# Sixteen unrolled attention batches against a loop over twelve of them

## The chip, the cores and the metric

The kernel runs on one core of one Trainium2 chip. The metric is the device time of one execution in microseconds (us). The engines are PE (matrix multiply; its weight loads are listed as PEld), DVE (vector), ACT (scalar and activation), POOL (GpSimd) and SP (which issues the DMAs). A q behind an engine's name (DVEq) means its sequencer: waits, register operations and branches.

## The reference, cut to what matters

The input x is 16 batches of 256 tokens by 256 features. The first half of the block is attention with 16 heads of 128: queries from x, one shared key and value projection scaled per head by a cumulative sum of decayed coefficients, rotary embedding, a causal softmax, and an output projection. The second half is a feed-forward part with 1024 hidden features whose weights are quantised to three values per group of 64.

```python
x = L0_attn_x                                  # (16, 256, 256) float32
x = x + _layernorm(attn(_layernorm(x), Wq, Wkv, Wkvh, Wg, Wout))
x = x + _layernorm(ffn(_layernorm(x), w_gate_up, w_proj))
# attn, for each batch and each of 16 heads of 128:
#   k = rope(kp * kh[head]);  v = vp * vh[head];  q = rope(x @ Wq.T)
#   o = softmax(mask(q @ k.T / sqrt(128))) @ v;   return o @ Wout.T
# ffn: h = silu(x @ Wg.T) * (x @ Wu.T);  return rms_norm(h) @ Wp.T
#   with Wg, Wu, Wp = ternary_quant(...), once for all batches
```

## The kernel before

The work is a hand-written software pipeline. Each of the five engines has its own program, and they meet only through semaphores that count up: an engine waits until a count has reached a threshold.

The attention part goes over 128 steps, eight for each of the 16 batches; a step takes one pair of heads (`HP` = 2, `PAIRS` = 8). Within a step every stage works on a different pair, behind by `LAG`: the projection of the queries (PE), their product with the cosine (DVE, L1372) and the swap of their halves (ACT, L1078 and L1079) on the newest pair; the product with the sine (POOL, L564), the sum (POOL, L574) and the scores (PE, L815 and L817) one behind; the row maxima come from DVE (L1384 to L1387); the exponentials (ACT, L1090 and L1092), the reciprocal of their sums (DVE, L1397) and the normalising product (POOL, L596) two behind; the transposes (PE, L832) with their split into a high and a low part (ACT L1108, DVE L1410) three, the product with the values and its split (ACT L1118, DVE L1419) four, and the output projection (PE, all split products are issued at L710) five behind. POOL also scales the keys (L585). Once per batch come the layer norms of the next batch's input and of the previous one's output, and the projections of keys, gates and values (`FRONT`, `TAIL`). SP loads, two steps ahead, one pair of coefficient rows into `kh_all`.

Beside this the ternary weights are made in six chunks; one chunk takes two batches (`ROUND` = 16 steps), with its stages at the steps listed in `WSTEP`. `chunk_at` says whether a stage of a chunk falls in the present step: `par` is the batch's parity, and the chunks lie in batches 1 to 12.

`over_batches` is called by every engine with its own function `batch(g0, par, steps)`, which writes out that engine's instructions for eight steps; `g0` is the number of the batch's first step. All thresholds and addresses are worked out from `g0` when the program is built: with a Python integer they are constants. The engine helper `pair_at` gives the pair of a stage and `at_least` drops waits that are trivially true.

The feed-forward part goes over 16 units, one per batch. `over_units` writes out the first and last of them and puts the ones between into a loop of the engine (`Fori`, L357), four rounds of two units, whose thresholds come from a register. Its first units run inside the last attention steps. L1142 (ACT, silu) and L1513 (DVE, product of gate and up) are steps of it, L958 is its transpose on PE, and L1533 a statistics operation on x tiles that are addressed by the unit's number.

Of the kernel before, what the change touches and what calls it, by code (L numbers as in the profile page):

```python
# [41 lines left out]
PAIRS = H // HP  # L42
STEPS = BATCH * PAIRS
# [24 lines left out]
WSTEP = dict(cast=0, sum=1, scale=2, above=3, below=3, decide=7, sign=7, change=9, finish=11, turn=15, copy=15, store_chunk=15, next_load=13)  # L68
CHUNKS = 6
ROUND = 2 * PAIRS  # L70
# [6 lines left out]
def sandwich_kernel(nc, x, wq, wkv, wkvh, wg, wout, wgu, wproj, rope, out):  # L77
    ctx = ExitStack()
    with ctx:
# [240 lines left out]

        def chunk_at(g0, par, s, stage):

            if isinstance(g0, int) and not PAIRS <= g0 < PAIRS + CHUNKS * ROUND:
                return None
            if WSTEP[stage] == s + (0 if par else PAIRS):
                return g0 if par else g0 - PAIRS

        def chunks_done(c0, of=1):
# [2 lines left out]

        def over_batches(eng, batch):

            for g0 in range(0, STEPS, PAIRS):
                batch(g0, g0 // PAIRS % 2, PAIRS)
            batch(STEPS, 0, DRAIN)

# [72 lines left out]
        def _(sp):  # L410
# [75 lines left out]
            for p in range(1, KH_LEAD):  # L486
                spread_kh(0, p)
            sp.dma_start(X[:, 2 * NT:half, :], tile_rows[:, 2 * NT:half, :]).then_inc(x_half, 16)
            over_batches(sp, batch)

            out_rows = out.rearrange("b (t p) e -> p (b t) e", p=P)
# [15 lines left out]
        def _(pool):  # L507
# [190 lines left out]
            queries_sin(0, LAG["rope"])  # L698
            queries_add(0, LAG["rope"])
            over_batches(pool, batch)  # L700
            over_units(pool, step)


        @block.tensor
        def _(pe):
# [168 lines left out]
            def weights_turn(g0, par, s):  # L874

                c0 = chunk_at(g0, par, s, "turn")
                if c0 is not None:
                    b = F_BANK.bitcast(BF16)
                    pe.wait_ge(wt_done, chunks_done(c0))
                    pe.wait_ge(v_lo_done, g0 + ROUND)  # L880
                    for a in range(FF // P):
                        last = nc.tensor.transpose(b[:, a * P:(a + 1) * P], w_tern[:, a * P:(a + 1) * P], ident_bf[:, :])
                    last.then_inc(wt_turned, ROUND)
# [116 lines left out]
            for i in range(2, LATER):  # L1000
                turn_weight(i)
            project_keys(0, 0)
            over_batches(pe, batch)
            over_units(pe, step)

# [712 lines left out]
```

## Time and profile before

| | |
|---|---|
| median of 3 runs | 1116.36 us (1114.75 to 1117.43) |
| profiled execution | 1116.36 us |
| its span, first to last instruction | 1114.6 us |
| PE, PEld busy | 95%, 90% |
| POOL, ACT, DVE busy | 84%, 78%, 75% |
| granted TensorE clock | 0.994 of full speed |

The profile is of one execution. A group's row names the line, the engine, what is written from what, and the times; the idle time of an engine stands with what ended it. The span is nearly the whole time; 1.8 us lie around it. Attention takes the first 890 us, the feed-forward part the rest.

### The profile page before, as it was taken

The numbers are of one execution on the slowest core, as the hardware profiler recorded it, in microseconds if no ns is written. First come the engines' busy times: TensorE is split into PE (matmuls) and PEld (weight loads), VectorE is DVE, ScalarE is ACT, GpSimd is POOL, SyncE is SP. The second block draws the span as 40 slices with busy tenths as digits, with TensorE's granted clock in tenths as the row PEclk, the third lists the DMA queues.
The fourth block names the chain that finished last, engine by engine and source line by source line (L and its number), as shares of the span: only waits on it lengthen the run. The fifth ranks groups of instructions, "written<-read, shape, count | busy, mean of one in ns | idle before, by whom it ended". The sixth has DMA issues, their size and how long they took to land.

```text
span 1114.6 us, 25542 instructions
## 1 busy us (share of the span) xinstructions
PE 1060.9 (95%) x8010; PEld 1007.1 (90%) x8010; DVE 841.2 (75%) x2854; ACT 866.7 (78%) x2386; POOL 933.7 (84%) x846
## 2 busy tenths in 40 slices
PE   6899999999999999999999999999999899999997
PEld 6799899889988999899989999999999799999997
DVE  5778887878788878887878897878777756566654
ACT  4887879787878797878888888888888767666674
POOL 3788989898899889988998899989898757767675
PEclk8999999999999999999999999999999999999998
DMA  7450112111111121111111111111131000000001
GB/s 256 163 165 27 50 50 65 36 43 59 50 39 44 53 58 40 39 50 58 39 44 44 67 40 58 43 45 39 39 106 30 1 2 21 21 19 19 19 20 39
DMA packets 35117, 58.46 MB, mean 52 GB/s; under 512 B 3137, under 2 KB 16001, under 8 KB 34689
## 3 DMA queue, kind: packets, MB, share of 16 engines
q1 hardware_dynamic: 34992, 56.96, 16.2%
q8 instruction: 59, 0.97, 0.3%
q14 instruction: 66, 0.53, 0.2%
HBM read 50.92 MB, written 9.18 MB: 54 GB/s over the span
## 4 chain that ended last, share of the span: by engine, by line
POOL 33%; PE 29%; issue 19%; DVE 11%; ACT 7%; DMA 1%; DVEq 0%; POOLq 0%; ACTq 0%
PE psum L710 10%; POOL arena L564 9%; PE psum L899 8%; POOL arena L574 8%; POOL arena L585 7%; POOL arena L596 7%; PE psum L929 4%; DVE pt_split L1410 2%; PE psum L815 2%; ACT arena L1090 2%; ACT arena L1092 1%; DVE arena L1372 1%; DVE o_lo L1419 1%; PE psum L817 1%; PE psum L909 1%
## 5 line engine op out<-in xcount | busy, mean ns | idle before, releaser
L596 POOL TENSOR_TENSOR arena<-arena 128x768 f32<-128x768 f32 x128 | 209.5, 1637 | 24.3 <-DVE arena L1397 23.7
L564 POOL TENSOR_TENSOR arena<-arena,tables 128x512 f32<-128x512 f32 x128 | 170.4, 1331 | 48.8 <-ACT arena L1079 48.1
L1410 DVE SCALAR_TENSOR_TENSOR pt_split<-psum,vh_col,pt_split 128x256 fp32r<-128x256 f32 (+1 forms) x512 | 186.9, 404 | 0.0
L574 POOL TENSOR_TENSOR arena<-arena 128x512 f32<-128x512 f32 x128 | 171.2, 1337 | 10.0
L585 POOL TENSOR_TENSOR arena<-arena 128x512 f32<-128x512 f32 x128 | 170.5, 1332 | 2.2 <-ACT arena L1054 1.8
L815 PE MATMUL psum<-arena 128*128 128x256 f32 x512 | 153.5, 381 | 11.1 <-POOL arena L574 10.9
L710 PE MATMUL psum<-wo_hi,o_hi 128*128 128x256 f32 x512 | 152.7, 298 | 0.0
L1078 ACT ACTIVATE arena<-psum 64x512 f32<-64x512 f32 x128 | 76.2, 595 | 97.7 <-DVE arena L1372 96.5
L1090 ACT ACTIVATE arena<-arena 128x256 f32<-128x256 f32 x256 | 129.5, 506 | 22.4 <-DVE arena L1387 17.5
L710 PE MATMUL psum<-xt_hi,wq_hi 128*128 128x256 f32 x512 | 146.3, 286 | 0.0
L710 PE MATMUL psum<-xt_lo,wq_hi 128*128 128x256 f32 x512 | 144.9, 283 | 0.0
L710 PE MATMUL psum<-xt_hi,wq_lo 128*128 128x256 f32 x512 | 144.7, 283 | 0.0
L710 PE MATMUL psum<-wo_hi,o_lo 128*128 128x256 f32 x512 | 144.4, 282 | 0.0
L710 PE MATMUL psum<-wo_lo,o_hi 128*128 128x256 f32 x512 | 143.7, 281 | 0.0
L710 PE MATMUL psum<-pt_split,vals_hi 128*128 128x512 f32 (+1 forms) x512 | 142.0, 358 | 1.2 <-DVE wo_lo L1268 1.2
L899 PE MATMUL psum<-xt_hi,wq_hi 128*128 128x256 f32 x512 | 128.3, 289 | 1.6 <-DVE xt_lo L1595 1.4
L899 PE MATMUL psum<-xt_lo,wq_hi 128*128 128x256 f32 x512 | 124.6, 282 | 0.0
L1108 ACT ACTIVATE pt_split<-psum,vh_col 128x256 fp32r<-128x256 f32 x256 | 121.6, 475 | 0.0
L1397 DVE RECIPROCAL arena<-arena 128x8 f32<-128x8 f32 x128 | 24.9, 194 | 123.6 <-ACT arena L1092 122.1
L602 POOL TENSOR_TENSOR wo_lo<-arena,wo_hi 128x512 fp32r<-128x512 f32 x64 | 88.8, 1396 | 27.9 <-ACT wo_hi L1149 27.8
L817 PEld LDWEIGHTS psum<-arena 128*128 128x128 f32 x512 | 97.1, 190 | 13.3
L1385 DVE CUSTOM_DVE_ANT_0 arena<-psum,mask 128x256 f32<-128x256 f32 x256 | 106.1, 415 | 0.0
(170 smaller groups left out, 3542.1 us busy)
## 6 DMA issues: line engine op xcount, KB each, us to landing
arena<-kh_rows SPq DMA_DIRECT2D x127, 256.0 KB, 3.3
out<-spare SPq DMA_DIRECT2D x15, 256.0 KB, 2.1
arena<-w_rows SPq DMA_DIRECT2D x6, 512.0 KB, 4.7
X<-L_attn_Wout SPq DMA_DIRECT2D x1, 2048.0 KB, 14.4
X<-L_attn_x SPq DMA_DIRECT2D x1, 2048.0 KB, 13.1
arena<-L_attn_Wq SPq DMA_DIRECT2D x1, 1536.0 KB, 10.0
X<-L_attn_x SPq DMA_DIRECT2D x1, 1536.0 KB, 9.5
w_rows<-L_ffn_w_gate_up SPq DMA_DIRECT2D x3, 512.0 KB, 8.1
```

The source lines that it names most:

```text
L564: nc.gpsimd.tensor_tensor(swap, swap, spread, ALU.mult).then_inc(q_sined, 1)
L574: nc.gpsimd.tensor_tensor(q_rot[p % 2], q_cos[p % 2], q_swap[p % 2], ALU.add).then_inc(q_roped, 1)
L585: nc.gpsimd.tensor_tensor(k_head[p % 2], keys[par].unsqueeze(1).to_broadcast([P, HP, N]), kh_all[p % 4], ALU.mult).then_inc(k_scaled, 1)
L596: nc.gpsimd.tensor_tensor(tb, tb, r.unsqueeze(3).to_broadcast([P, HP, 3, P]), ALU.mult).then_inc(p_ready, 1)
L710: last = nc.tensor.matmul(o, a, b, start=start and i == 0, stop=stop and i == len(passes) - 1, skip_group_check=skip)
L815: nc.tensor.matmul(sj[:, 0:2 * P], q[:, j, P:N], kt[:, j, :], start=True, stop=True, skip_group_check=True)
L817: nc.tensor.matmul(sj[:, 2 * P:3 * P], q[:, j, 0:P], kt[:, j, 0:P], start=False, stop=True, skip_group_check=True).then_inc(s_ready, 1)
L899: last = nc.tensor.matmul(bank[c % 2 * 2 + half][:, j * N:(j + 1) * N], wgu_t[:, k, col:col + P], part[:, k, :], start=n == 0 and j == 0, ...
L1090: nc.scalar.activation(tb[:, j, 0:2 * P], tb[:, j, 0:2 * P], ACT.Exp, scale=-1.0, bias=nmax[p % 4][:, 2 * j:2 * j + 1], accum_out=rsum[p % ...
L1108: nc.scalar.activation(pt_hi[p % 2][:, j * N:(j + 1) * N], b[:, 0:N], ACT.Copy, scale=vh[:, 0, h:h + 1])
L1385: nc.vector.tensor_tensor_reduce(tb[:, j, 0:2 * P], S_BANK[j][:, 0:2 * P], mask[:, :], -1.0, -MASKED, ALU.add, ALU.min, nmax[p % 4][:, 2 * ...
L1410: last = nc.vector.scalar_tensor_tensor(pt_lo[p % 2][:, o], b[:, i], vh[:, t, h:h + 1], pt_hi[p % 2][:, o].bitcast(F32), ALU.mult, ALU.sub ...
```

## The change

The batches are no longer all written out. Batch 0 is written out as before; batches 1 to 12 become a loop of six rounds of two batches on each engine, in which `g0` is a register; batches 13 to 15 and the drain are written out. `chunk_at` now asks whether `g0` is a register instead of comparing its number, which picks the same twelve batches. In the loop, thresholds and addresses that depend on `g0` are computed by register operations, and the round ends with a compare-and-branch. Nothing else differs.

```diff
         def chunk_at(g0, par, s, stage):
 
-            if isinstance(g0, int) and not PAIRS <= g0 < PAIRS + CHUNKS * ROUND:
-                return None
-            if WSTEP[stage] == s + (0 if par else PAIRS):
+            if not isinstance(g0, int) and WSTEP[stage] == s + (0 if par else PAIRS):
                 return g0 if par else g0 - PAIRS
...
         def over_batches(eng, batch):
 
-            for g0 in range(0, STEPS, PAIRS):
+            batch(0, 0, PAIRS)
+            with eng.Fori(PAIRS, PAIRS + (CHUNKS - 1) * ROUND + 1, ROUND) as g0:
+                batch(g0, 1, PAIRS)
+                batch(g0 + PAIRS, 0, PAIRS)
+            for g0 in range(PAIRS + CHUNKS * ROUND, STEPS, PAIRS):
                 batch(g0, g0 // PAIRS % 2, PAIRS)
             batch(STEPS, 0, DRAIN)
```

## Rows read from the trace of the kernel before

**Rows 1.** The page: span, busy time, chain that ended last by engine.

```profile
span 1114.6 us, 25542 instructions
...
PE 1060.9 (95%) x8010; PEld 1007.1 (90%) x8010; DVE 841.2 (75%) x2854; ACT 866.7 (78%) x2386; POOL 933.7 (84%) x846
...
POOL 33%; PE 29%; issue 19%; DVE 11%; ACT 7%; DMA 1%; DVEq 0%; POOLq 0%; ACTq 0%
```

**Rows 2.** Windows of a batch: length, busy PE, PEld, DVE, ACT, POOL (operations), clock, DMA.

```profile
187.60:242.60 55.00, 52.21 (x385) 48.81 (x385) 47.04 (x165) 44.07 (x132) 49.74 (x40) 1.00 0.14 40
...
729.60:782.40 52.80, 51.72 (x385) 48.94 (x386) 41.24 (x156) 43.92 (x131) 46.06 (x39) 1.00 0.15 41
```

**Rows 3.** Waits between 87 and 730 us: us in total, times, longest.

```profile
DVE arena L1397 <- ACT arena L1092: 92.2, 77, 2.8
ACT arena L1078 <- DVE arena L1372: 75.0, 78, 2.2
...
PE psum L832 <- DVE pt_split L1410: 15.9, 36, 0.6
```

**Rows 4.** Sequencer instructions of the feed-forward loop: ns min/median/max, first and last start.

```profile
L357 PEldq COMPARE_BRANCH  x4: 76/214/243, 994.6 to 1074.0; - x4
...
L357 DVEq COMPARE_BRANCH  x4: 50/56/68, 997.4 to 1076.8; - x4
...
L1533 DVEq FUSED_REGOPS  x16: 57/60/71, 976.8 to 1069.5; - x16
```

**Rows 5.** DMA view, 190 to 296 us: instruction queues, packets, MB, share.

```profile
q8 instruction: 6, 0.10, 0.4%
q14 instruction: 8, 0.07, 0.2%
```

**Rows 6.** DMA view: every queue between 1000 and 1070 us; two issues of the page.

```profile
q1 hardware_dynamic: 1360, 1.31, 5.6%
...
arena<-kh_rows SPq DMA_DIRECT2D x127, 256.0 KB, 3.3
...
kh_rows<-arena SPq DMA_DIRECT2D x16, 16.0 KB, 1.4
```

**Rows 7.** Windows: a round of the feed-forward loop, and the unrolled unit behind it.

```profile
1020.95:1047.42 26.47, 26.20 (x218) 25.79 (x217) 16.20 (x34) 17.88 (x35) 19.01 (x27) 1.00 0.06 20
...
1073.86:1086.92 13.06, 13.06 (x110) 12.88 (x109) 7.22 (x13) 9.88 (x19) 11.63 (x14) 1.00 0.07 23
```

**Rows 8.** Window of two attention batches, and the waits of line 291 in it.

```profile
187.60:296.10 108.50, 104.38 (x777) 98.20 (x777) 88.98 (x323) 89.06 (x263) 98.52 (x79) 1.00 0.15 48
...
L291 PEldq EVENT_SEMAPHORE  x54: 51/51/51, 187.8 to 295.4; - x54
L291 DVEq EVENT_SEMAPHORE  x54: 21/21/1269, 187.9 to 296.0; - x54
```

**Rows 9.** Timelines of ACT and DVE around 408 us: start, length, [idle before].

```profile
407.04 0.59 ACT L1078 ACTIVATE arena<-psum 64x512 f32<-64x512 f32 x1
407.65 0.59 ACT L1079 ACTIVATE arena<-psum 64x512 f32<-64x512 f32 x1
...
410.50 0.20 DVE L1397 RECIPROCAL arena<-arena 128x8 f32<-128x8 f32 x1 [1.06 <-ACT arena L1092]
```

**Rows 10.** Timelines: one hand-over in the feed-forward loop, one in the unrolled tail.

```profile
1027.49 0.59 ACT L1142 ACTIVATE arena<-psum 128x512 f32<-128x512 f32 x1
...
1028.28 0.69 DVE L1513 TENSOR_TENSOR arena<-arena,psum 128x512 f32<-128x512 f32 x1 [2.79 <-ACT arena L1142]
...
1080.38 0.59 ACT L1142 ACTIVATE arena<-psum 128x512 f32<-128x512 f32 x1
...
1081.01 0.69 DVE L1513 TENSOR_TENSOR arena<-arena,psum 128x512 f32<-128x512 f32 x1 [2.61 <-ACT arena L1142]
```

**Rows 11.** Line 596 on POOL: ns min/median/max; its group on the page.

```profile
L596 POOL TENSOR_TENSOR arena<-arena x128: 1459/1472/2458, 33.3 to 882.5; 128x768 f32<-128x768 f32 x128
...
L596 POOL TENSOR_TENSOR arena<-arena 128x768 f32<-128x768 f32 x128 | 209.5, 1637 | 24.3 <-DVE arena L1397 23.7
```

## The prediction

> **What bounds the kernel now.** I read the head of the page first. The profiled execution took 1116.36 us, of which 1114.6 is the span of the trace; it equals the median of the three runs (1116.36), so the sum below is made against 1116.4. The matrix engine is busy 95% of the span, POOL 84%, ACT 78%, DVE 75%, and the chain that ended last changes hands all the time (POOL 33%, PE 29%, issue 19%, DVE 11%, ACT 7%): no single engine is the bound, it is a ring of hand-overs between four nearly full engines [rows 1]. Next the windows of one batch each. A batch of eight steps takes 55.0 us when it carries the heavy half of the weight work and 52.8 once that work is over; a step is 6.6 to 6.9 us [rows 2]. Then the waits of the twelve batches that will be in the loop: DVE waits for ACT's exponentials (L1397 behind L1092, 92.2 us in 77 waits, 1.2 each), ACT for DVE's cosine product (L1078 behind L1372, 75.0 in 78), and PE, 15.9 in 36, for DVE's split (L832) [rows 3]. PE's own waits are small beside 640 us, so what reaches the time must first eat into these. The reader is to see that the steps are tied by a ring: DVE's maxima, ACT's exponentials, DVE's reciprocal and cosine, ACT's swap, POOL, PE.
>
> **How much of a delay reaches the time.** The windows give a measure of it: the heavy half of the weight work puts 5.8 us more on DVE than a batch without it (47.04 against 41.24) and lengthens the batch by 2.2 us (55.0 against 52.8) [rows 2]. So something under 0.4 of small work spread over DVE comes through; I take 0.3 to 0.4 for small delays spread over steps.
>
> **The change, part by part.**
>
> *The arithmetic and the order.* Nothing is removed. Batch 0 stands alone, six rounds of two batches (1 to 12) run from one copy of the code, batches 13 to 15 and the drain follow. The weight stages fall in the same twelve batches at the same steps. Every matmul, activation and tensor operation is issued as often and in the same order on its engine, and each engine loops by itself, with no barrier between engines. Cost: nothing, no cover needed.
>
> *Six comparisons with branch on each engine, five taken.* The kernel before has such a loop in its last stage, over the units of the feed-forward part (L357), and the trace times it: 50 to 68 ns for a compare-and-branch on DVE, 76 to 243 on PE; a register operation on DVE is some 60 ns, and two go with the branch [rows 4]. That is at most 0.4 us per edge, spent by the sequencer while the engine still has queued work. Six edges: under 2.4 us on PE with no cover, taken as nothing, because the feed-forward loop shows no gap from it (below).
>
> *Fetching the code at each taken edge.* This is the first real term. Straight code is fetched ahead: over two batches the instruction queues brought 6 packets of 16 KB on one (PE) and 8 of 8 KB on the other (the rest), with no engine idling for it [rows 5]. In the feed-forward loop, between 1000 and 1070 us, no instruction packet is moved at all [rows 6]: a body that is small (34 DVE, 35 ACT, 27 POOL operations and 218 matmuls in a round of 26.47 us [rows 7]) stays on the engine. The new body is far larger. Counted over two batches, 323 DVE operations and at least 54 waits, 263 operations on ACT and 79 on POOL, 777 matmuls with their 777 weight loads and 54 waits on PE [rows 8], and the register operations come on top. PE's 1608 in the 0.10 MB of its six packets are some 62 bytes each, so a packet of 8 KB holds about 130: that is three to four packets for DVE, more than two for ACT, about one for POOL, and six to seven of 16 KB for PE. If the first of them is gone when the engine jumps back, it must be fetched while the engine runs dry. The trace has no such event. From below it costs nothing (the body stays) or the 1.4 us in which the smallest DMA of the kernel, 16 KB, lands; from above the 3.3 us of a 256 KB one [rows 6]. I take the middle of the two, 2.4 us. It is partly covered. ACT's last operations of a step are the two halves of the swap, 1.2 us of queued work at 407.04 to 408.24, directly ahead of the exponential that a new round begins with [rows 9]: 1.2 us net. DVE's first instruction of a step is the reciprocal that waits 1.06 us for ACT anyway [rows 9], and it has its queue besides, so its own fetch is hidden or runs beside ACT's. POOL's body is small and PE ran ahead of the branch in the feed-forward loop. Late next are DVE's reciprocal, then POOL's normalising product and PE's transposes. 5 x 1.2 = 6 us; the ends are 0 and 5 x 3.3 = 16.5.
>
> The Trainium skill (Runtime: NRT & Kernel Launch, Instruction fetch mechanics) says that prefetch is only sequential and that a taken branch to code outside the two current pages waits for its page. The empty instruction queues of the small loop agree with it as far as they go; its 16 KiB pages are 8 KB packets on the second queue here, and the trace decides. By the rule alone every one of the five edges would stall DVE and ACT, by the observed retention of a small body perhaps none; the sum above lies between them.
>
> *Waits against registers.* The second term. In the loop each new threshold is a register operation, and where one instruction waits for several things, the first wait is put on the register operation for the next threshold. The feed-forward loop shows what that costs. In looped code ACT's L1142 ends at 1027.49 + 0.59 = 1028.08 and DVE's L1513 starts at 1028.28, 0.20 us later; in the unrolled tail L1142 ends at 1080.38 + 0.59 = 1080.97 and L1513 starts at 1081.01, 0.04 later [rows 10]. So 0.16 to 0.17 us on a hand-over that is waited for. It doesn't strike every time: a round of two looped units takes 26.47 us, and the unrolled unit behind the loop 13.06, so the loop costs 0.35 per round, or 1.3% [rows 7], two or three such delays among its dozens of waits. In the attention steps several awaited hand-overs have more than one condition: L1078 (cosine done, rotated copy free), L574, L815, L1118. From below the cost is nothing, if the thresholds are computed while the engine is busy; from above one hand-over per step on the path, 96 x 0.17 = 16.3 us. I take one per step on the ring, times the 0.3 that comes through: 96 x 0.17 x 0.3 = 4.9 us. If the slack of rows 3 were gone it would be the 16.3.
>
> *Addresses from registers.* The x tiles of one batch are addressed from g0 (stats, norm, residual): a few register operations of some 60 ns [rows 4] at three places per batch, 12 batches, on DVE, ACT and POOL beside running work. SP computes the address of 16 loads and 2 stores per round; each load is issued two steps (13 us) ahead and lands in 3.3 [rows 6]. Nothing; 12 x 0.2 = 2.4 us if the cover were gone.
>
> Sum: 1116.4 + 6 + 4.9 = 1127.3, forecast **1127 us**, 1.0% slower.
>
> **The rivals.**
>
> *A. All of it is hidden.* The body's head is still there or its fetch is covered by the queues, and thresholds are ready in time. For it: no visible gap at the feed-forward edges, 1.2 us of wait in front of L1397. Against it: DVE's body is nine times as large as that one [rows 7, 8], and the ring has no free engine. Time: 1116.4 + 0 to 2, so 1117.
>
> *B. The edge is dear.* The fetch takes 3.3 us and nothing covers it, because PE's body, over 100 KB, is fetched anew as well, and a stalled PE (95% busy) can't catch up; and hand-overs come through at 0.6. Time: 1116.4 + 16.5 + 96 x 0.17 x 0.6 = 1142.7. For it: PE's six to seven packets, 16 KB each. Against it: PE's branch ran ahead of its matmuls. The skill's page on fetching (above) speaks for this one, since by it no large body is kept.
>
> *C. It gets faster.* One mechanism: the small delays shift DVE against POOL. L596 takes 1.46 us undisturbed and up to 2.46 beside certain DVE work, 1.64 in the mean of 128 [rows 11]: 0.17 of collision per step. If the looped steps settle so that it vanishes, POOL gains 96 x 0.17 = 16 us, of which a third (its share of the chain) would count: 5.4 us, to 1111 if nothing else costs. It decides only if both terms above come to less than 5.4 us. Nothing in the trace says that the shift goes this way.
>
> **How the numbers follow.** About 0.2% (2.2 us) is what a measurement of this kernel can tell from no change. The forecast case (both terms, 1119 to 1135) gets 0.47; A 0.17; B and what lies between (1135 to 1150 and over) 0.25; C 0.11. Slower by over 0.2% holds the forecast and B and a sliver of A: 0.76. Within 0.2%: 0.13. Faster: 0.11. The range leaves out most of C and the far end of B: 1114 to 1147. The likeliest case's own range is 1119 to 1135.
>
> **What the profile after would show.** Register operations on all queues between 85 and 740 us, with a branch line at the line of the new loop, six per engine, about 108 us apart. Fetches of instruction packets at each edge on ACT and DVE if the first term is right; the idle time of L1090 or L1397 then has five long waits of 1 to 3 us marked "issue", and none if A holds. Windows of a round inside the loop 109.5 to 111 us against 108.3 now. Between edges a step grows by 0.05 us; if it grows by 0.15 or more the second term was too small. PE's matmuls, POOL's and DVE's durations stay as they are; if L596's mean falls, C is at work. The prediction is wrong if batches 13 to 15 or the feed-forward part change, since nothing there was touched.

## The result and the profile after

The looped kernel takes 1130.67 us in the median (1130.1 to 1133.14, 4 runs), the kernel before beside it on the same chip 1116.89 (1114.75 to 1118.52, 4 runs). The ratio is 1.0129, with an interval of 1.0105 to 1.0152: 1.3% slower, 14 us where 10.6 were forecast. The profiled execution took 1129.83 us.

The page of the looped kernel, its head, busy times and chain by engine:

```profile
span 1128.0 us, 26834 instructions
...
PE 1063.4 (94%) x8010; PEld 1005.8 (89%) x8010; DVE 845.8 (75%) x2854; ACT 868.0 (77%) x2386; POOL 933.9 (83%) x846
...
PE 31%; POOL 21%; issue 21%; DVE 14%; ACT 10%; DMA 2%; DVEq 1%; ACTq 0%; POOLq 0%; SPq 0%
```

The operations of every engine are as many as in [rows 1]; 1292 sequencer instructions were added. DVE is busy for 4.6 us more with the same operations, which is the first sign that some of them take longer.

The windows: two looped rounds, then one of the batches behind the loop (columns as in [rows 2]).

```profile
188.50:299.40 110.90, 104.95 (x778) 98.28 (x777) 90.10 (x323) 89.42 (x263) 98.62 (x78) 1.00 0.15 46
299.40:410.40 111.00, 104.99 (x778) 98.30 (x778) 90.12 (x323) 89.44 (x263) 98.56 (x78) 1.00 0.15 46
743.50:796.20 52.70, 51.57 (x382) 48.46 (x382) 40.92 (x158) 43.57 (x130) 46.10 (x40) 1.00 0.14 42
```

Two batches took 108.50 before [rows 8] and take 111 now; the last batch takes 52.7, as in [rows 2]. All of the time is lost in the loop. The granted clock is 1.00 in the windows of either kernel.

How much is lost there is best read between two marks of the same work: POOL's normalising product of the first step and of the last. Its group over the whole trace, in the kernel before [rows 11], goes from 33.3 to 882.5, 849.2 us. In the looped kernel:

```profile
L598 POOL TENSOR_TENSOR arena<-arena x128: 1459/1472/2453, 30.9 to 895.4; 128x768 f32<-128x768 f32 x128
```

895.4 - 30.9 is 864.5 us, 15.3 more. The first product comes at about 31 or at 33.4 us in different executions, looped or not (31.4 in before_gates below, 33.5 in after_hint); that difference lies ahead of the first product and is no part of the change. I call the distance between the two products the stretch and give it for every experiment, because it leaves that scatter out.

The same product step by step shows where the 15.3 us are. POOL's timeline around the jump from the second round to the third and the start of the third, before (L596) and after (L598):

```profile
283.43 1.47 POOL L596 TENSOR_TENSOR arena<-arena 128x768 f32<-128x768 f32 x1
289.95 1.47 POOL L596 TENSOR_TENSOR arena<-arena 128x768 f32<-128x768 f32 x1
296.29 1.47 POOL L596 TENSOR_TENSOR arena<-arena 128x768 f32<-128x768 f32 x1
302.68 1.48 POOL L596 TENSOR_TENSOR arena<-arena 128x768 f32<-128x768 f32 x1
```

```profile
285.48 1.47 POOL L598 TENSOR_TENSOR arena<-arena 128x768 f32<-128x768 f32 x1
292.96 1.47 POOL L598 TENSOR_TENSOR arena<-arena 128x768 f32<-128x768 f32 x1 [0.79 <-DVE arena L1399]
299.55 1.47 POOL L598 TENSOR_TENSOR arena<-arena 128x768 f32<-128x768 f32 x1 [0.29 <-DVE arena L1399]
307.27 1.49 POOL L598 TENSOR_TENSOR arena<-arena 128x768 f32<-128x768 f32 x1
```

The three steps took 6.52, 6.34 and 6.39 us and take 7.48, 6.59 and 7.72. The first two hold the jump: 0.96 + 0.25 = 1.2 us, about 1.3 with a remainder in the steps behind. The third loses 1.33 where there is no jump at all. The pattern repeats: about 1.3 us at each of five taken branches, 1.33 to 1.37 us at the third of these steps in each of the six rounds, 0.4 us at the entry. 5 x 1.3 + 6 x 1.35 + 0.4 = 15.0 of the 15.3. The other steps of the loop agree to 0.04 us, but for one in the middle of each round, 0.07 to 0.16 longer, and one that is 0.28 shorter, once. These are two causes, and I take them in turn.

**At the jump.** The sequencers' rows of the loop's line (L333) between 280 and 300 us (instruction, ns, start), the waits of ACT that are put down to issue, over the whole trace, and the instruction queue from 287.5 to 291.9 us:

```profile
L333 DVEq COMPARE_BRANCH  x1: 68/68/68, 287.6 to 287.6; - x1
L333 ACTq COMPARE_BRANCH  x1: 45/45/45, 288.0 to 288.0; - x1
L333 DVEq FUSED_REGOPS  x1: 74/74/74, 290.4 to 290.4; - x1
L333 ACTq FUSED_REGOPS  x1: 47/47/47, 290.6 to 290.6; - x1
```

```profile
ACT arena L1092 <- issue: 5.2, 5, 1.1
```

```profile
q14 instruction: 4, 0.03, 1.9%
```

A branch of 45 to 68 ns, and the next instruction 2.6 us (ACT) and 2.8 us (DVE) later, with packets of instructions in between. ACT and DVE on their timelines:

```profile
288.16 0.59 ACT L1081 ACTIVATE arena<-psum 64x512 f32<-64x512 f32 x1
288.77 1.02 ACT L1134 ACTIVATE arena<-psum 128x1024 bf16<-128x1024 bf16 x1
290.78 0.51 ACT L1092 ACTIVATE arena<-arena 128x256 f32<-128x256 f32 x1 [0.98 <-issue]
```

```profile
292.68 0.20 DVE L1399 RECIPROCAL arena<-arena 128x8 f32<-128x8 f32 x1 [3.40 <-ACT arena L1094]
```

ACT's queued work ends at 288.77 + 1.02 = 289.79; then it stands for 0.98 us. DVE's first operation of the round has to wait for ACT's exponentials until 292.68, so its own 2.8 us end long before that. PE has no such event: in the DMA view of 165 to 730 us its instruction queue (q8) has no row, where the kernel before moved 33 packets in the same stretch. The queue of the other engines (q14) moves 50 packets there, where it moved 38 before: ACT and DVE fetch their bodies again in every round (it moves 49 and 46 with one of the two looped alone, 30 with neither, in the experiments below).

**One step of each round.** DVE's timeline at the start of the third round's third step, before (L1397, L1345, L1285) and after:

```profile
296.01 0.20 DVE L1397 RECIPROCAL arena<-arena 128x8 f32<-128x8 f32 x1 [1.67 <-ACT arena L1092]
296.13 0.21 DVE L1345 COPY vh_col<-psum 128x64 f32<-128x64 f32 x1
296.26 0.15 DVE L1285 SCALAR_TENSOR_TENSOR arena<-arena 128x2 f32<-128x2 f32 x1
```

```profile
299.27 0.20 DVE L1399 RECIPROCAL arena<-arena 128x8 f32<-128x8 f32 x1 [1.75 <-ACT arena L1094]
299.45 0.23 DVE L1347 COPY vh_col<-psum 128x64 f32<-128x64 f32 x1
299.59 1.46 DVE L1287 SCALAR_TENSOR_TENSOR arena<-arena 128x2 f32<-128x2 f32 x1
300.96 1.21 DVE L1434 TENSOR_REDUCE arena<-arena 128x16 f32<-128x1024 bf16 x1
```

```profile
L291 DVEq FUSED_REGOPS  x3: 46/46/46, 218.5 to 299.3; - x3
```

`bias_x` is a product of two columns (128x2). Before, it started 0.25 us behind the reciprocal, 0.03 us ahead of POOL's product (296.29), and took 0.15 us. Now it starts 0.32 behind, 0.04 us after POOL's product (299.55), and takes 1.46, as long as that product, and DVE's next operation starts 1.3 us late. What has moved it is a register operation of 46 ns ahead of `copy_vh` (L1347), the last row: the copy waits for two things there, one instruction in the unrolled code, and in the loop one of the two waits is put on the register operation that works out the other's threshold. The copy thus starts 0.17 us behind the reciprocal's start instead of 0.12. It isn't PE, whose transposed coefficients the copy needs: in all six rounds they are there 0.07 us or more before the reciprocal starts.

The Trainium skill (SBUF — State Buffer, "SBUF: two separate sides") has the rule for this: a DVE operation with two inputs in SBUF and a GpSimd operation that reads SBUF lock each other out of a shared pair of ports, whichever starts first holding it to its end. `bias_x` has two such inputs, the copy before it has one, in PSUM. The rows agree with it: 0.15 us when it starts 0.03 ahead, 1.46 when it starts 0.04 after. How closely the recorded starts decide it, before_late2 shows below.

### The profile page after: what moved, and what is told of

Its sections match the earlier page's. It is cut to its first block, busy times and chain, and to the rows that moved or that the text cites. A ratio compares the mean times of both kernels' runs of the same rounds, so it can differ in the third digit from the quotient of the medians.

```text
span 1128.0 us, 26834 instructions
## 1 busy us (share of the span) xinstructions
PE 1063.4 (94%) x8010; PEld 1005.8 (89%) x8010; DVE 845.8 (75%) x2854; ACT 868.0 (77%) x2386; POOL 933.9 (83%) x846
## 3 DMA queue, kind: packets, MB, share of 16 engines
q1 hardware_dynamic: 34992, 56.96, 15.6%
## 4 chain that ended last, share of the span: by engine, by line
PE 31%; POOL 21%; issue 21%; DVE 14%; ACT 10%; DMA 2%; DVEq 1%; ACTq 0%; POOLq 0%; SPq 0%
PE psum L712 10%; PE psum L901 8%; POOL arena L566 6%; POOL arena L576 5%; POOL arena L587 5%; PE psum L931 4%; POOL arena L598 3%; DVE pt_split L1412 3%; PE psum L817 3%; ACT arena L1094 2%; DVE arena L1374 2%; ACT arena L1092 2%; DMA X<-L_attn_x 1%; PE psum L819 1%; DVE o_lo L1421 1%
## 5 line engine op out<-in xcount | busy, mean ns | idle before, releaser
L598 POOL TENSOR_TENSOR arena<-arena 128x768 f32<-128x768 f32 x128 | 209.5, 1637 | 30.4 <-DVE arena L1399 29.9
L576 POOL TENSOR_TENSOR arena<-arena 128x512 f32<-128x512 f32 x128 | 171.1, 1337 | 10.6 <-POOL arena L566 1.1
L1080 ACT ACTIVATE arena<-psum 64x512 f32<-64x512 f32 x128 | 76.2, 595 | 106.3 <-DVE arena L1374 105.7
L1092 ACT ACTIVATE arena<-arena 128x256 f32<-128x256 f32 x256 | 129.5, 506 | 27.0 <-DVE arena L1389 18.9
```

The source lines that it names most:

```text
L576: nc.gpsimd.tensor_tensor(q_rot[p % 2], q_cos[p % 2], q_swap[p % 2], ALU.add).then_inc(q_roped, 1)
L598: nc.gpsimd.tensor_tensor(tb, tb, r.unsqueeze(3).to_broadcast([P, HP, 3, P]), ALU.mult).then_inc(p_ready, 1)
L1092: nc.scalar.activation(tb[:, j, 0:2 * P], tb[:, j, 0:2 * P], ACT.Exp, scale=-1.0, bias=nmax[p % 4][:, 2 * j:2 * j + 1], accum_out=rsum[p % ...
```

## The experiments

In the twelve kernels below, "stretch" is the distance defined above (849.2 before, 864.5 after); the ratio is against the kernel before on the same chip.

### Which engine's loop costs what: one engine looped at a time

Each engine walks the batches by itself and the semaphores' counts are the same in either form, so one engine can loop while the others are written out. `looped` is True for ACT alone (loop_act), for DVE alone (loop_dve), or for PE, POOL and SP (loop_rest). Lines are 7 higher there than before.

```diff
-        def over_batches(eng, batch):
+        def over_batches(eng, batch, looped):
 
-            for g0 in range(0, STEPS, PAIRS):
+            first = 0
+            if looped:
+                batch(0, 0, PAIRS)
+                with eng.Fori(PAIRS, PAIRS + (CHUNKS - 1) * ROUND + 1, ROUND) as g0:
+                    batch(g0, 1, PAIRS)
+                    batch(g0 + PAIRS, 0, PAIRS)
+                first = PAIRS + CHUNKS * ROUND
+            for g0 in range(first, STEPS, PAIRS):
                 batch(g0, g0 // PAIRS % 2, PAIRS)
```

> Only ACT runs the loop over batches 1 to 12; the other four engines keep the unrolled code. Theory (two separate costs: ACT's empty queue at each taken edge, about 1.4 us, and on DVE a lost race of one small operation against POOL once per round, about 1.35 us): the five edges cost 7 us and the race is not lost, so 1124 us, with five waits of about 1 us of L1090 marked issue, and the small operation of L1285 in odd batches stays near 0.15 us. Rival 1 (the edge is DVE's fetch, since the gap before the reciprocal is the longest): 1117. Rival 2 (register thresholds cost a little at every hand-over on every engine): about a quarter of the 14 us, 1120, spread over all steps.

Measured: 1122.24 us, ratio 1.0040 (1.0025 to 1.0056), stretch 33.3 to 888.7 = 855.4, 6.2 more than before. The expected 1124 was 2 us too high. ACT's wait at the jump, and the waits for issue over the whole trace:

```profile
290.54 0.51 ACT L1097 ACTIVATE arena<-arena 128x256 f32<-128x256 f32 x1 [0.84 <-issue]
```

```profile
ACT arena L1097 <- issue: 4.4, 5, 1.0
```

The five waits are there with ACT's loop alone. They cost (6.2 - 1.4) / 5 = 0.97 us each; the 1.4 is the other loss, which struck once, in the first round (the small product at 79.23 took 1.45 us there). DVE has no register operation in this kernel: its copy waited for PE's coefficients, which came 0.09 us after the reciprocal's start, where they had come 0.01 ahead of it in the profiled execution of the kernel before. So the first meeting can be lost without a loop, and it is lost in the same way in three unrolled kernels below.

> Only DVE runs the loop. Theory: DVE fetches at each edge too, but it waits for ACT's exponentials there anyway, so the edge is hidden; the race is lost in each of the six rounds (the operation of L1287 takes 1.4 us in place of 0.15): 6 x 1.35 = 8.1, so 1125 us. Rival 1 (DVE's fetch is the edge's cost): 1125 + 7 = 1132. Rival 2 (costs spread over hand-overs): 1120 to 1122 with no step longer by more than 0.2 us.

Measured: 1125.19, ratio 1.0081 (1.0057 to 1.0104), stretch 33.2 to 891.2 = 858.0, 8.8 more. As expected. The reciprocal behind the jump and the meeting in the round's first batch, DVE's timeline:

```profile
292.54 0.20 DVE L1404 RECIPROCAL arena<-arena 128x8 f32<-128x8 f32 x1 [2.30 <-ACT arena L1099]
...
299.06 0.20 DVE L1404 RECIPROCAL arena<-arena 128x8 f32<-128x8 f32 x1 [1.67 <-ACT arena L1099]
299.24 0.23 DVE L1352 COPY vh_col<-psum 128x64 f32<-128x64 f32 x1
299.38 1.45 DVE L1292 SCALAR_TENSOR_TENSOR arena<-arena 128x2 f32<-128x2 f32 x1
```

At the jump DVE still waits for ACT and not for its own code, and the two steps there grow by 0.02 to 0.1 us together. The lost meeting is there in all six rounds: 6 x 1.35 = 8.1 of the 8.8.

> PE, POOL and SP run the loop, ACT and DVE the unrolled code. Theory: PE's body stays on the engine (no 16 KB instruction packets between 165 and 730 us), POOL's too, register operations are hidden: 1117 us, no change. Rival 2 (spread costs): some 1120 to 1125. If PE's edge counted it would show five steps longer by 1 us or more.

Measured: 1116.56, ratio 1.0002 (0.9987 to 1.0016), stretch 849.8. As expected: three engines in a loop, PE with its 1600 instructions among them, cost nothing that can be measured in the time. The two steps at each jump do grow, by 0.09 us together in the mean. The DMA view of 165 to 730 us has one packet for PE:

```profile
q14 instruction: 30, 0.25, 0.2%
q8 instruction: 1, 0.02, 0.0%
```

The stretches of the three add up to 6.2 + 8.8 + 0.6 = 15.6, against 15.3 for all of them together. But the first meeting is lost in loop_act and in loop_dve, so 1.4 us stand twice in that sum, and without them it is 14.2. The two steps at a jump add up to 1.07 (ACT alone) + 0.07 (DVE alone) + 0.09 (the rest) = 1.23, against 1.29 for all engines.

### The meeting taken away in the looped kernel

after_swap puts `bias_x` in front of `copy_vh`, straight behind the reciprocal. The two have nothing to do with each other.

```diff
                     c0 = vh_at(g0, s)
+                    c1 = front_at(g0, s, "norm")
+                    if c1 is not None:
+                        bias_x(c1)
                     if c0 is not None and not is_first(c0, 0):
                         copy_vh(c0, par)
-                    c0 = front_at(g0, s, "norm")
-                    if c0 is not None:
-                        bias_x(c0)
```

> The changed kernel with one pair of DVE operations exchanged in step 1 of a batch: the bias of the next batch's norm (the small operation that loses the race) before the copy of the value coefficients. Theory: the small operation then starts before POOL's normalising product in each round and takes 0.15 us, the 8.1 us go: 1130.7 - 8.1 = 1122.6 us. Rival (the long operation is a symptom of a late DVE, not the cause; the time is lost in register operations): 1130, with the loss moved to the next operation.

Measured: 1123.27, ratio 1.0065 (1.0042 to 1.0088), stretch 30.7 to 887.1 = 856.5, which is 8.0 less than in the looped kernel, where 6 x 1.35 = 8.1 were expected. DVE in the third round:

```profile
296.17 0.20 DVE L1399 RECIPROCAL arena<-arena 128x8 f32<-128x8 f32 x1 [1.74 <-ACT arena L1094]
296.29 0.13 DVE L1287 SCALAR_TENSOR_TENSOR arena<-arena 128x2 f32<-128x2 f32 x1
296.45 0.23 DVE L1347 COPY vh_col<-psum 128x64 f32<-128x64 f32 x1
```

The small product is over before POOL's starts (296.45). What is left over the kernel before, 7.3 us, is the five jumps, the entry and the small remainders.

> The unrolled kernel with the same pair of DVE operations exchanged. Theory: the race was not lost there in the odd batches, and in the even ones the small operation is half hidden, so nothing or a few tenths: 1116 to 1117 us. Rival (the exchange is a gain by itself, and explains the gain in the looped kernel): 1109 to 1111.

The same edit in the kernel before: 1116.85, ratio 0.9997 (0.9985 to 1.0009), stretch 849.3. No gain where the meeting was won already, so the edit's 8 us in the looped kernel are not a gain that it brings by itself.

### The meeting lost on purpose, without a loop

If 0.06 us of delay is what costs 8 us, the unrolled kernel must lose them to a delay of any kind in the same place. A fill that nobody reads goes ahead of `copy_vh` in the six odd batches, of one column (before_late):

```diff
                     if c0 is not None and not is_first(c0, 0):
+                        if par and c0 < PAIRS + CHUNKS * ROUND:
+                            nc.vector.memset(small3[:, 52:53], 0.0)
                         copy_vh(c0, par)
```

> The unrolled kernel with one DVE operation of 60 ns (a fill of a single unused column) ahead of the copy of the value coefficients, in batches 1, 3, 5, 7, 9 and 11 alone. Theory: it makes the small operation behind the copy start after POOL's normalising product and wait for it, 6 x 1.35 = 8.1: 1125 us from 0.4 us of added work. Rival (only the loop's registers do this): 1116.9 to 1117.5.

Measured: 1116.79, ratio 0.9995 (0.9982 to 1.0009). A miss: the fill was too small. It ran beside the reciprocal, moved the small product from 0.249 to 0.265 us behind it, still ahead of POOL's 0.28, and the meeting was lost in one round of six (stretch 851.1, 1.9 more). That one, the first, was not lost by the fill: the copy waited for PE's coefficients, 0.13 us after the reciprocal's start. before_late2 fills 96 columns of another tile, `nc.vector.memset(spare[:, 0:96], 0.0)`, in the same place.

> As before_late, but the added DVE operation fills 96 columns, since the fill of one column ran under the reciprocal and moved the small operation by 0.015 us only (start 0.265 us after the reciprocal, POOL's product at 0.28, race still won in five of six rounds and no time lost). This fill moves it past 0.28 us. Theory (whoever starts first has the way into memory, and the loser waits for the whole POOL operation): the small operation of L1285 takes 1.4 us in all six rounds and the kernel 1116.9 + 6 x 1.35 = 1125 us. Rival (only a register wait makes it slow): 1117.5.

Measured: 1124.77, ratio 1.0063 (1.0043 to 1.0084). The time is the expected 1125, but the kernel before took 1118.13 beside it, so the fill costs 6.6 to 7 us in place of 8.1. In the profiled execution (1122.33, stretch 855.1, 5.9 more) the meeting was won in two rounds and lost in four, and that shows the boundary. The first round shown is a won one, the second a lost one; DVE's timeline:

```profile
188.48 0.20 DVE L1397 RECIPROCAL arena<-arena 128x8 f32<-128x8 f32 x1 [1.67 <-ACT arena L1092]
188.66 0.14 DVE L1612 MEMSET spare<- 128x96 f32 x1
188.79 0.15 DVE L1285 SCALAR_TENSOR_TENSOR arena<-arena 128x2 f32<-128x2 f32 x1
...
297.05 0.20 DVE L1397 RECIPROCAL arena<-arena 128x8 f32<-128x8 f32 x1 [1.67 <-ACT arena L1092]
...
297.35 1.46 DVE L1285 SCALAR_TENSOR_TENSOR arena<-arena 128x2 f32<-128x2 f32 x1
```

and POOL's:

```profile
188.76 1.51 POOL L596 TENSOR_TENSOR arena<-arena 128x768 f32<-128x768 f32 x1
...
297.33 1.47 POOL L596 TENSOR_TENSOR arena<-arena 128x768 f32<-128x768 f32 x1
```

The small product starts 0.31 and 0.30 us behind the reciprocal, 0.02 to 0.03 behind POOL's start in both. Once it takes 0.15 us and POOL's product 1.51 (0.04 more than its 1.47), once 1.46. There is no loop in this kernel, so the loop isn't needed for the loss, only the delay is. Three of the four were lost by the fill, the first again by PE's coefficients (0.17 us late). Each lost round has one step that is 1.33 to 1.38 us longer; in the two won rounds, which have the same fill, that step is no longer than before (0.03 us). So it is the lost meeting that costs, and not the fill: 4 x 1.35 = 5.4 of the 5.9.

### The jump announced

after_hint tells each engine of the jump back before it comes, with one instruction at the top of each round (BRANCH_PREFETCH_HINT in the trace); after_both has the swap as well.

```diff
-            with eng.Fori(PAIRS, PAIRS + (CHUNKS - 1) * ROUND + 1, ROUND) as g0:
+            with nc.Fori(PAIRS, PAIRS + (CHUNKS - 1) * ROUND + 1, ROUND, engines=[eng.engine], hint_back_edge=True) as g0:
```

> The changed kernel, whose loop now announces its jump back at the top of each round, so that the first code block can be fetched before it is needed. Theory: the 1.35 us per edge are ACT waiting for its first block; they go, 5 x 1.35 = 6.8, so 1130.7 - 6.8 = 1124 us, and the waits of L1092 marked issue vanish. The lost race stays (L1287 1.4 us). Rival (the edge's cost is the branch and the first register operations, not the fetch): 1130 to 1131.

Measured: 1126.37, ratio 1.0077 (1.0048 to 1.0106), stretch 33.5 to 893.0 = 859.5: 5.0 us less than the looped kernel, where five jumps at 1.3 would be 6.5, and 2.4 us above the expected 1124. In the DMA view of the jump (287 to 294 us) no instruction packet is moved any more, and L1092 has no wait for issue in the whole trace. The view of 165 to 730 us shows more: there isn't one instruction packet in it, where the looped kernel without the hint moved 50. So the loop's head isn't fetched early, as was meant; nothing is fetched at all, and the bodies of ACT and DVE, 385 and 471 instructions in a round with those of their sequencers, stay on the engines. Their size is thus not what has them fetched again without the hint. How the hint keeps them the runs don't show.

Instead ACT has a wait for issue behind the loop, 14 us after the branch that isn't taken (729.3):

```profile
743.65 0.60 ACT L1080 ACTIVATE arena<-psum 64x512 f32<-64x512 f32 x1 [1.50 <-issue]
```

An instruction packet starts just ahead of this wait (at 741.98), so it looks as if code behind the loop was now what wasn't there; that is argued from the times. Part of the 1.5 us is made up in the next steps (1.47 lost, then 0.8 and 0.27 gained).

> The changed kernel with the announced jump and the exchanged pair of DVE operations. Theory (the two costs are the whole difference and add up): 1123.3 - 6.8 = 1116.5 us, the time of the unrolled kernel. Rival (something else is left, register thresholds above all): 1119 to 1122.

Measured: 1120.24, ratio 1.0022 (1.0011 to 1.0033), stretch 852.6, 3.5 more than before. A miss by 3.7 us, on the side of the rival that something is left. Step by step it is 1.0 at the entry of the loop, 0.3 at its end (1.27 lost, 0.96 gained) and about 0.4 at each of the five jumps, in pieces of 0.09 to 0.17 over the steps behind it. What these pieces are was not tried. The two steps at a jump make up 0.19 of them, and in the same two steps loop_dve grows by 0.07 and loop_rest by 0.09 with no wait of ACT, so most of the 0.19 comes with looping the other engines, whatever ACT does.

### A version that beats both

There may be other such meetings. `gates_one` (L1308, 32x256) takes 0.28 us in its shortest case and 1.38 in the middle one, about as long as POOL's product beside it; its group in the kernel before:

```profile
L1308 DVE TENSOR_SCALAR arena<-arena x16: 281/1378/1379, 13.5 to 802.6; 32x256 f32<-32x256 f32 x16
```

before_gates moves it from the step's beginning, just behind the start of POOL's product, to its end. No loop.

```diff
                         keys_cos(c0)
-                        gates_one(c0)
...
                     if c0 is not None:
+                        gates_one(c0)
                         decays(c0)
```

> The unrolled kernel with another small DVE operation moved away from a collision that it has in 15 of 16 batches: gates_one (L1308, 1.38 us in the median, 0.28 at best) goes from right behind the reciprocal and the key product, where POOL has just begun a long operation, to the end of the same step, ahead of the decays that need it. Theory: 1.1 us less on DVE's busy part of the ring per batch, of which 0.35 to 1 reaches the time: 1100 to 1111 us. Rival: the end of that step is already the long one (a reciprocal of 1.7 us there), so the gain is eaten: 1113 to 1117.

Measured: 1112.08, ratio 0.9955 (0.9942 to 0.9968), 0.4% faster than the kernel before and the fastest version of all; between the two expectations. The group now:

```profile
L1308 DVE TENSOR_SCALAR arena<-arena x16: 281/632/896, 13.1 to 802.5; 32x256 f32<-32x256 f32 x16
```

It saves 0.75 us of DVE's time per batch, of which 0.25 us per batch reaches the time, since DVE has waits of its own to eat it [rows 3]. The stretch is 846.9, with one lost meeting of 1.4 in it.

That it waits for POOL here too can be read from where it ends. The same batch in the kernel before, then in before_gates:

```profile
316.55 1.47 POOL L596 TENSOR_TENSOR arena<-arena 128x768 f32<-128x768 f32 x1
316.78 1.38 DVE L1308 TENSOR_SCALAR arena<-arena 32x256 f32<-32x256 f32 x1
...
317.77 1.28 POOL L564 TENSOR_TENSOR arena<-arena,tables 128x512 f32<-128x512 f32 x1
318.56 0.64 DVE L1308 TENSOR_SCALAR arena<-arena 32x256 f32<-32x256 f32 x1
```

It starts 0.23 us into POOL's product before and 0.79 into another product of POOL's now, and ends 0.14 us after POOL's in both. In all 15 batches where the two meet, of either kernel, that distance is 0.14 to 0.15 us, and without a product of POOL's beside it (at 13.5) it takes 0.28. So the move didn't take the meeting away; it starts later into it. The operation has one input in SBUF and not two, so it is another case than `bias_x`, with the same effect.

after_three is the looped kernel with hint, swap and this move; after_acthint has the hint on ACT alone (`hint_back_edge=hinted`, True in ACT's call only).

> The looped kernel with the announced jump, the exchanged pair and gates_one at the end of its step. Theory: the gain of before_gates (about 5 us) comes on top of after_both: 1120.2 - 5 = 1115 us, a fifth of a per cent above or below the unrolled kernel. Rival (the gain depends on the order in which DVE and POOL meet, and is not had in the loop): 1119 to 1121.

Measured: 1116.24, ratio 0.9991 (0.9978 to 1.0004), stretch 847.7. That is 1.2 us above the theory's 1115, and no change against the kernel before.

> The same with the jump announced on ACT alone. Theory: ACT's fetch is the one that reaches the time, DVE's is hidden behind the exponentials once ACT is on time, PE and POOL need none: as after_three, 1114 to 1115 us, or a little less, since the other four engines save the instruction that announces. Rival (DVE's fetch comes out once ACT's is gone): 5 x 0.5 to 1.2 us more, 1117 to 1121.

Measured: 1115.45, ratio 0.9982 (0.9970 to 0.9995), stretch 847.2. This is 0.5 us above the upper end of the theory's 1114 to 1115, and below the rival's 1117. With the hint on ACT alone there is no wait for issue on L1080 behind the loop, where after_three, hinted on every engine, has one of 1.3 us; so that wait doesn't come from ACT's own hint alone, and which other engine's brings it was not tried. DVE's fetch, unhinted, stays hidden (27 packets are moved between 165 and 730 us): a looped kernel as fast as the unrolled one, though 3 us behind the unrolled one with the same move.

## Why the prediction was right, and where it was right by chance

**What bounds the kernel: held.** No engine was the bound: delays of 1.0 and 1.3 us on ACT and DVE, which are busy for 75 to 78% of the span, reached the time whole, because the ring passes them on.

**Nothing for order, branches and addresses: held.** loop_rest has the branches of three engines and SP's and POOL's addresses and measures 1.0002. DVE's and ACT's branches are 45 to 68 ns.

**Fetching the code, 6 us forecast: held, in place and nearly in size.** The step said 2.4 us of fetch less 1.2 us of ACT's queued work, five times, with DVE's own fetch hidden behind its wait for ACT. Measured: 2.6 us from branch to next instruction on ACT, cover up to 289.79, 0.98 us of idle, five times, and 1.0 (ACT alone) to 1.3 (all engines) in the time; 2.8 us on DVE, hidden in loop_dve. So 6.5 us and 0.4 at the entry. That the net came so near is in part luck: the 2.4 was the middle between two data transfers and not a time of fetching, and the cover was 1.7 us (L1081 and then L1134 of the weight work, 288.05 to 289.79) where two halves of the swap had been counted. And the step gave the wrong reason. It took the bodies of ACT and DVE for too large to stay; after_hint, without a packet in the loop, shows that they can stay, and PE's, over three times as large, stays without a hint. The five waits marked issue stand on ACT's first exponential, as written. PE was not fetched anew (no packet from 165 to 730 us), which puts out rival B.

I misread the Trainium skill there. It (Runtime: NRT & Kernel Launch, "Instruction fetch mechanics") states that a jump outside the resident pages waits for its page, and the trace agrees for ACT and DVE; but it also gives PE four times the store of the others, 128 KiB. PE's body of some 100 KB fits into that, and the empty queue agrees. Rival B took the rule of the two pages for PE as well, which the page leaves open and the trace refutes.

**Waits against registers, 4.9 us forecast: the size came out at 8.1, and the step behind it failed.** The step was "one per step on the ring, times the 0.3 that comes through": many small delays, spread, a step growing by 0.05 us. Measured between jumps: no step grows by more than 0.04, but for one in each round, by 1.35, and another by some 0.1. The register operation does delay an awaited hand-over, by 0.06 us here, and everywhere else the ring swallows that whole; in this one place it decides which of two operations goes first. before_late2 shows the same loss without any register, after_swap takes it away with all registers in place. That the sum came out near is chance here: the 4.9 us priced a cost that isn't there, and the cost that is there was in no term. A term that was a delay times a fraction should have been a count of close meetings times the length of the longer operation.

**Rival C named the right meeting, and with the wrong sign.** It wrote that small delays shift DVE against POOL and that this might gain. The shift is there and lost 8.1 us, and before_gates shows that a shift by intent can gain: 2.3 us of stretch, 3.7 without the meeting that it lost. The Trainium skill's rule on the shared ports (above) prices such a meeting at the whole of the other operation, which I had not looked up. The trace of before had it to be read: `bias_x` starts 0.03 us ahead of POOL's product.

**Rival A, all hidden: false** by the interval. Batches 13 to 15 and the feed-forward part are unchanged, as they had to be. The round came to 110.9 to 111.0 us, the upper end of the 109.5 to 111 given.

What stays open: what the 0.07 and 0.09 us are that a jump costs with DVE or the other three looped, and the 0.4 per jump that stays with the hint; how the hint keeps a body on its engine; which hint brings the wait behind the loop. The entry is uncertain by 0.3 us, by which one step near the loop's entry was longer in the profiled execution of the kernel before than in the four other unrolled kernels and in loop_act.

## What to carry to other kernels

Before a loop replaces written-out code, look at the engine on the path: is its code fetched again at the jump (the instruction queues of the DMA view tell; its size alone doesn't), and how much queued work lies ahead of the jump. Everything else about the loop was free here, but for the order of two operations. Announcing the jump on that engine alone took the fetch away. Then look for operations of DVE and POOL that start within 0.1 us of each other, for there a delay of 50 ns can be worth the whole of the longer one, as it was here. A forecast that spreads a small delay evenly can come out near the right sum for the wrong reason; the experiment that loops one engine at a time tells.

## What the runs showed of the hardware that was not expected

- A DVE product of 128x2 with both inputs in SBUF took 0.15 us when it started 0.03 us ahead of POOL's product, 1.45 to 1.46 when it started 0.03 to 0.04 after it, and either when it started 0.022 to 0.025 after it (before_late2).
- A DVE operation of 32x256 that adds a constant, 0.28 us alone, ended 0.14 us after the product of POOL's beside which it started, whether it had started 0.23 or 0.8 us into it.
- A body of 1600 PE instructions (about 100 KB) stayed on the engine over five jumps; those of ACT and DVE, 385 and 471 instructions with their waits and register operations, did not, and took 2.6 and 2.8 us from branch to next instruction. With the jump announced they stayed too.
- Announcing the jump took these 2.6 us away, and every instruction packet between 165 and 730 us with them. Announced on all engines it came with 1.3 to 1.5 us of idle ACT once behind the loop, announced on ACT alone with none.
- Between jumps, some 1200 more sequencer instructions added nothing by themselves.
